# Wide filler matmuls and bfloat16 degree sums in the node network of a two-layer graph network

## The reference, cut to what matters

```
h  = relu(layernorm(x))
# layer 0: an edge network, summed over edges, then a node network
e1 = relu([edge_attr, h[src], h[dst]] @ We1 + be1)
e2 = relu(e1 @ We2 + be2)
agg = segment_sum(e2 @ We3 + be3, dst)
g  = relu([h, agg] @ Wn1 + bn1)
g  = relu(g @ Wn2 + bn2)
x  = x + (g @ Wn3 + bn3)
# layer 1: eight heads of attention over the same edges, both ends exchanged
h  = relu(layernorm(x))
q  = softmax(h[src] @ u - h[dst] @ u + c)
x  = x + sum over m of segment_sum(q[:, m] * weight * h[dst], src) @ w[m] + b
```

## Time and profile before

| | |
|---|---|
| runs shown | 2416.97 us median of 3 (2416.3 to 2418.75) |
| profiled execution | 2419.39 us |
| its span, first to last instruction | 2417.6 us |
| mean granted TensorE clock | 0.696 of full speed |
| first loop ends, node network begins | 1164.7 us |
| second loop's first load issued | 1261.8 us |

### The profile page before, as it was taken

The page is one execution under the profiler, slowest core; times in us unless marked ns, Lnnn a source line. Parts: engine busy times, 40 slices in busy tenths (PEclk is TensorE's granted clock), DMA queues, the critical chain, the costliest instruction groups (busy, mean ns, idle before and its releaser), DMA issues.

```text
span 2417.6 us, 50381 instructions
## 1 busy us (share of the span) xinstructions
PE 1718.0 (71%) x9991; PEld 1194.3 (49%) x9991; DVE 1317.0 (54%) x5192; ACT 555.0 (23%) x1977; POOL 1680.1 (69%) x1700
## 2 busy tenths in 40 slices
PE   4688889998888899898946555556556556556555
PEld 3355555555555555555534444445445444445444
DVE  5133332333322333322138888888888888888885
ACT  2233333333333333333111111111111111111110
POOL 2677777777777777777336777677777777777773
PEclk8798997989999988988655555555555555555555
DMA  3433333333333333333043333333333333333332
GB/s 73 98 70 68 69 68 69 71 68 71 68 68 69 69 67 71 69 68 68 20 77 94 91 94 92 90 94 93 90 94 92 91 94 92 92 93 93 90 94 60
DMA packets 269590, 191.00 MB, mean 79 GB/s; under 512 B 199089, under 2 KB 242640, under 8 KB 269566
## 3 DMA queue, kind: packets, MB, share of 16 engines
q0 software_dynamic: 66800, 113.26, 20.1%
q1 hardware_dynamic: 200822, 75.78, 13.4%
q10 hardware_dynamic: 1944, 1.69, 0.3%
HBM read 183.85 MB, written 6.69 MB: 79 GB/s over the span
## 4 chain that ended last, share of the span: by engine, by line
DVE 30%; issue 24%; PE 17%; DMA 11%; POOL 10%; DVEq 6%; ACT 1%; SPq 0%; ACTq 0%; POOLq 0%
POOL X L553 10%; DMA X<-table_src,slot_s 8%; DVE EQW L1103 4%; DVE EQW L1109 3%; PE bank L1325 3%; DVE OT L943 3%; PE bank L1308 3%; PE bank L1316 3%; PE bank L1334 2%; DVE EX L1149 2%; DVE r L1141 2%; DVE OE L1154 2%; DVE r L1136 2%; DVE r L1145 2%; DVEq L1168 2%
## 5 line engine op out<-in xcount | busy, mean ns | idle before, releaser
L561 POOL DMA_INDIRECT G<-table_node_and_list,slot_s x825 | 805.1, 976 | 362.2 <-issue 209.7
L553 POOL DMA_INDIRECT X<-table_src,slot_s x825 | 834.3, 1011 | 300.6 <-issue 264.9
L1443 PE MATMUL bank<-Q,G 125*64 125x128 f32 x1650 | 413.8, 422 | 181.7 <-DVE Q L1162 181.6
L957 DVE TENSOR_TENSOR sT<-sT,bank 65x16 f32 x275 | 46.2, 168 | 710.7 <-PE bank L1344 675.6
L1443 PEld LDWEIGHTS bank<-Q,G 125*64 125x64 f32 x1650 | 312.7, 221 | 194.6 <-issue 126.1
L1308 PE MATMUL bank<-filler 128*128 128x384 bf16 x1100 | 385.3, 350 | 2.2 <-issue 2.2
L1454 PE MATMUL bank<-R,w_z 65*64 65x64 f32 x1104 | 133.5, 315 | 270.0 <-DVE sT L1170 270.0
L943 DVE TENSOR_SCALAR OT<-KBT,base_p 48x375 bf16<-48x375 int32 x550 | 234.2, 426 | 92.7 <-DMA KBT<-in_dst 43.3
L1325 PE MATMUL bank<-XT,w_ex 128*64 128x375 f32 x550 | 263.9, 566 | 0.0
L1454 PEld LDWEIGHTS bank<-R,w_z 65*64 65x64 f32 x1104 | 122.5, 224 | 274.1 <-issue 274.1
L1316 PE MATMUL bank<-ident,X 125*128 125x125 f32 x825 | 151.8, 297 | 144.2 <-DMA X<-table_src,slot_s 114.4
(11 more groups left out here) (165 smaller groups left out, 1952.9 us busy)
## 6 DMA issues: line engine op xcount, KB each, us to landing
KBT<-in_dst SPq DMA_DIRECT2D x550, 70.3 KB, 2.1
X<-in_edge_attr SPq DMA_DIRECT2D x275, 93.8 KB
X<-table_src,slot_s POOLq DMA_INDIRECT x825
G<-table_node_and_list,slot_s POOLq DMA_INDIRECT x825
BW<-table_dst_parts SPq DMA_DIRECT2D x275, 6.0 KB
UW<-table_logit_src_parts SPq DMA_DIRECT2D x275, 0.8 KB, 1.6
table_node_and_list<-sm SPq DMA_DIRECT2D x1, 1562.5 KB
table_dst_parts<-G SPq DMA_DIRECT2D x1, 1171.9 KB
```

The costliest lines, as they stand in the source:

```text
L553: pool.indirect_dma_start(X[:, j, q, D:2 * D], None, tA, bass.IndirectOffsetOnAxis(ap=slot_s[:, j, q:q + 1], axis=0)).then_inc(gat_a[0][j] ...
L561: pool.indirect_dma_start(G[:, j, q, :], None, tH, bass.IndirectOffsetOnAxis(ap=slot_s[:, j, q:q + 1], axis=0)).then_inc(g_gather[j], 16)
L1443: last = pe.matmul(bank[2 + j % 2][0:D, 0:WM], G[0:P, j, q, 0:D], Q[:, j % 2, q].rearrange("p m n -> p (m n)"), start=(q == 0), stop=(q == ...
```

## The change

The filler array becomes 512 columns wide, and the first loop keeps using 384 of them. In the node network each of the three groups of products in a step gets a filler of 512 columns into its bank, behind the waits: 7 for each layer, 21 in all. VectorE copies `sT` to bfloat16 (in G) and one column of the identity to `unit`, and the 25 degree matmuls take these; `degrees()` waits for that copy. `degrees()` moves from step 0 to step 1, behind the second layer's product there, and `degree_sums()` from step 1 to step 2, behind the second layer's product there.

```
-        filler = sb("filler", [128, 384], BF16)
+        filler = sb("filler", [128, 512], BF16)
+        unit = sb("unit", [DC, 1], BF16)
...
+        counts_b = G[0:DC].rearrange("p j q f -> p (j q f)").bitcast(BF16)[:, 0:N]
...
+        counts_ready = sem("counts_ready")
...
+            dve.wait_ge(sT_ready, 1)
+            dve.tensor_copy(unit[:], ident[0:DC, D:DC])
+            dve.tensor_copy(counts_b, sT[:]).then_inc(counts_ready, 1)
+
             degs = [0]
...
-            def fill(to):
-
-                pe.matmul(to[:, 0:384], filler[:, 0:128], filler[:], start=True, stop=True)
+            def fill(to, n=384):
+
+                pe.matmul(to[:, 0:n], filler[:, 0:128], filler[:, 0:n], start=True, stop=True)
...
             def degrees():
+                pe.wait_ge(counts_ready, 1)
                 for b in range(NB):
-                    last = pe.matmul(bank[7][0:P, b:b + 1], sT[:, b * P:(b + 1) * P], ident[0:DC, D:DC],
+                    last = pe.matmul(bank[7][0:P, b:b + 1], counts_b[:, b * P:(b + 1) * P], unit[:],
                                      start=True, stop=True)
                 last.then_inc(deg_pe, 1)
...
                     if c >= 2:
                         done_act(pe, ("g1", c - 2))
+                    fill(bank[c % 2], 512)
                     pe.matmul(bank[c % 2][0:D, 0:hi - lo], wn1h[:], hT[:, lo:hi], start=True, stop=False)
...
-                if k == 0:
-                    degrees()
-                if k == 1:
-                    degree_sums()
                 if 1 <= k <= NCH:
                     c, (lo, hi) = k - 1, chunk_cols(k - 1)
                     done_act(pe, ("g1", c))
                     if c >= 2:
                         done_act(pe, ("g2", c - 2))
+                    fill(bank[2 + c % 2], 512)
                     pe.matmul(bank[2 + c % 2][0:D, 0:hi - lo], wn2[:], hT[:, lo:hi], start=True, stop=True
                               ).then_inc(pe_step, 1)
+                if k == 1:
+                    degrees()
+                if k == 2:
+                    degree_sums()
                 if k >= 2:
                     c = k - 2
                     done_act(pe, ("g2", c))
                     if c >= 2:
                         done_dve(pe, ("x1", c - 2))
+                    fill(bank[4 + c % 2], 512)
                     for n, b in enumerate(chunk_blocks(c)):
```

## The result

| | before | after |
|---|---|---|
| median of 21 runs each | 2416.83 us | 2422.17 us |
| range of the runs | 2412.89 to 2420.31 | 2418.88 to 2425.89 |
| profiled execution, span | 2419.39, 2417.6 | 2419.29, 2417.5 |

The ratio is 1.0023, with an interval of 1.0016 to 1.0029: 5.3 us slower, 3.9 to 7.0 by the interval. The forecast was 2418.3 us, in 2415 to 2421.5.

What follows compares the result with a forecast made beforehand. Bound: the second loop starts when SP's queue drains, which follows POOL's gathers and the degree sums. Sums 1.3 us later (-10.6 + 6.7 + 2.0 + 3.2) give 2420.7 us profiled, 2418.3 us for the runs, range 2415 to 2421.5.

Steps and rivals of the forecast that it cites:

- so the second loop starts 1.3 us later: Between the loops: degree sums end 1.3 us later, scan, gathers and queue stay unchanged, so the second loop starts that much later.
- costed them at nothing: VectorE's copies of sT and the unit column, about 2.1 us, end before PE reaches the degrees, so the wait costs nothing.
- The network's term: End of the degree sums: -10.6 + 6.7 (products) + 2.0 (fillers) + 3.2 (bfloat16 degrees) = +1.3 us.
- the bounds given: For the end of the degree sums: from 0.0 to +2.9 us.
- The x1 leg: Network, layer norms, logits: 1.4 us earlier up to the fourth x1, about 1 us back after; net near zero, not the bound.
- Half clock for the whole network: TensorE's granted clock stays 0.50 throughout the network despite the fillers, since the idle wait before it is not removed.
- The rival with full clock: Fillers keep or bring back full clock in the network: start_i 8.7 us earlier, run 2408.3 us; chance 0.13.
- The two legs: Gathers of the lists, then SP's full queue, set the second loop's start; network, layer norms and logits need only issue transfers in time.
- the slack: Node rows and logit parts are issued 1 to 5 us before their turn on SP's queue; the later queue adds 1.3 us.
- Degree matmuls one by one: Rival: the 25 degree matmuls do not overlap their weight loads, 11.4 us, run 2426.5 us; chance 0.06.

Runs made afterwards that it cites:

- act_copies: The whole change, with the two copies on ScalarE ahead of its relus instead of on VectorE: 2412.42 us, 2410.53 before, ratio 1.0009.
- aligned: The whole change, but with the unit column allocated behind all other arrays: 2419.53 us, 2415.35 before, ratio 1.0017.
- unmoved: The change with the bfloat16 degrees back at step 0 and their sums at step 1: 2417.17 us, 2415.17 before, ratio 1.0011.
- bridge: The change plus seven fillers ahead of the wait for sT and one ahead of every fifth degree matmul: 2405.64 us, 2410.53 before, ratio 0.9982.
- again: The change itself measured once more, beside other kernels on one chip: 2419.99 us, 2415.17 before, ratio 1.0021.
- degrees_only: The change without the 21 fillers of the network: 2418.01 us, 2415.35 before, ratio 1.0004.

## Why the prediction was wrong

**The size failed, not the direction**: a loss of 1.3 us was forecast and one of 5.3 us came. The step that failed is "so the second loop starts 1.3 us later", which I took for the whole effect: it made the end follow from the start alone and left the second loop's length as it was. VectorE's copies make that loop 1.5 us longer, on every profile, and I had costed them at nothing because they hide behind PE in the network. They do hide there; their price is in the loop that follows them. That is 1.5 of the 4 us by which the forecast fell short; the next term gives 0.2 to 0.5 more, and the rest, some 2 us by the medians, stays open.

**The network's term was right in kind and too small.** In the forecast five fillers cost 2.0 us and the second layer's products 1.67 each, since a weight load could hide under a filler. Measured were 0.43 to 0.54 for a filler and 1.86 for the product behind it, so the four products cost 1.86 + 1.86 + 1.67 + 1.86 = 7.25 and not 6.7, and the five fillers about 2.4 (0.43 for the first, had it run at half clock, then 0.47, 0.54, 0.45, 0.54). With 2.76 for the degrees (forecast 3.2) the sum is -10.6 + 7.25 + 2.4 + 2.76 = 1.8 us, within the bounds given. The profile after shows 0.1 us only because the clock fell 2.2 us into the network; `act_copies`, where the clock fell 0.5 us after the network's start, shows 1.5.

**The sum** is then 1.5 to 1.8 us of network and 1.5 us of loop, 3.0 to 3.3 us. The two comparisons of the change gave 5.3 (3.9 to 7.0) and 5.1 (2.9 to 7.2), and `aligned`, which differs by the place of one array, 4.1 (1.7 to 6.5). The last two intervals hold the sum, the first does not quite: some 0.6 us at least stay open. The x1 leg, which `unmoved` shows close behind and the dip in the change's own queue closer still, may be the later one in executions that were not profiled; no profile here shows a later start from it for the change.

**Half clock for the whole network** was right but for its first 2.2 us: 0.50 from 1165.1 on, as before. The reason given, the idle time ahead, is borne out: `bridge` fills it, adds five fillers, and the clock stays. The rival with full clock failed for this change; in `bridge`, with the entry covered, its clock came. The Trainium skill ("TensorE: Matmul & The Clock Gate", Part 1) says that activity releases the throttle; the activity that these fillers add did not, in 56.9 us. The Trainium skill says on the same page, in the section "HAM oscillation — how this bites in real kernels", that waits between bursts of matmuls let the clock fall back; `bridge`, which fills one such wait and adds five fillers, agrees.

**The two legs** were read rightly: 41.86 us from the lists to the first load with a queue that is full but for the dip, and 97.2 us from the first filler to that load, where 97.1 + 1.3 was forecast. **The x1 leg** was sized too low. I had it 1.4 us earlier up to the fourth x1 (its bounds add up to 4.4 earlier and 1.3 later, not 5 and 1); it was 2.5 earlier there in the profile (1208.94 - 1162.80 = 46.1 for 48.6), 1.7 of it from the full clock at the start. But the first node rows go out 2.7 us later (1232.64 - 1162.80 = 69.8 for 1231.89 - 1164.72 = 67.2), and the slack was to become 1.3 us wider, not to be used up. For one, the layer norm waits (timelines, VectorE, before and then after):

```profile
1219.17 0.25 DVE L841 RECIPROCAL st<-st 125x16 f32<-125x16 f32 x1 [0.38 <-ACT st L647]
...
1213.17 1.22 DVE L842 TENSOR_REDUCE st<-ab 125x16 f32<-125x1024 f32 x1
1216.45 0.25 DVE L844 RECIPROCAL st<-st 125x16 f32<-125x16 f32 x1 [2.06 <-ACT st L650]
```

The square root is on ScalarE behind the last relu of the second layer, and that relu behind PE's last fillers. I had looked at PE's and DVE's order and not at ScalarE's. The larger part comes behind it, in the 32 logit matmuls of the first half (timelines, PE, before and then after):

```profile
1226.77 4.50 PE L1417 MATMUL bank<-w_u,hT 65*125 65x16 f32 x32 [0.66 <-ACT hT L769]
...
1225.12 6.90 PE L1428 MATMUL bank<-w_u,hT 65*125 65x16 f32 x32 [0.66 <-ACT hT L772]
```

Their granted clock was 0.79 on average before and 0.50 after. That is not the change's doing alone: `aligned` had 4.38 us there and `again` 6.90.

**Degree matmuls one by one** fell: 2.76 us for 25, 0.11 each, though each shows 245 ns alone.

## What to carry to other kernels

Fillers behind the gap in which the clock fell did not bring it back here; with fillers in the gap it stayed. Put them there, and first ask whether that stretch sets the end at all. When two legs meet in a queue, work out which one fills it; here bfloat16 degrees at the front with their sums right behind gave 8 us without a filler in the network, and full clock without that move gave some 4 to 5. A few instructions added to an engine ahead of a tight loop can change the loop: compare its period per turn, engine by engine, and try such work on an engine whose loop has slack.

## What the runs showed of the hardware

- Two copies and a wait on VectorE ahead of a loop of 1156 us made it 1.5 us longer (nine profiles against five) and opened a wait of 0.25 us at one place in each turn, 64 times in 1050 us; with the copies on ScalarE it was gone.
- Network products of 65 rows with three fillers of 512 columns a step went at 0.50 for 56.9 us after the clock had fallen, and at 1.00 for 33.2 us where it had not (`bridge`, with seven fillers ahead and five among the degrees).
- Indirect gathers of 0.94 us that began during one of two VectorE instructions of 1.22 us (L837 and L846 in `degrees_only`) took 1.22 to 1.82 us, in four kernels: each ended 2.04 to 2.07 us after the start of that instruction.
- 25 bfloat16 matmuls of one column with 125 weight columns took 2.76 us at half clock, as against 10.59 in float32.
